# Local attention of a six-part decoder: another order of the work within each group of heads, on all four engines

## The chip, the core and the metric

One core of a Trainium2 chip runs the whole program in one launch. The metric is device time in microseconds (us), the median of the runs shown. TensorE multiplies, VectorE, ScalarE and GpSimd do the element-wise work, and SyncE only starts transfers. In the profile they are called PE (with PEld for its weight loads), DVE, ACT, POOL and SP.

## The reference, cut to what matters

Sixteen sequences of 128 tokens with 256 features pass through six layers: a recurrent mixer, grouped attention over a context, a dense and expert network, local attention (the one changed here), cross attention and a gated network. Each is added to its input after a normalisation. The local attention is:

```python
HEADS, KV_HEADS, HEAD_DIM = (16, 4, 128)
WINDOW, ROPE_THETA, EPS = (64, 10000.0, 1e-06)
q = (x @ Wq.T).reshape(B, T, H, Dh).transpose(0, 2, 1, 3)
k = (x @ Wk.T).reshape(B, T, Hkv, Dh).transpose(0, 2, 1, 3)
v = (x @ Wv.T).reshape(B, T, Hkv, Dh).transpose(0, 2, 1, 3)
q = _rms_norm(q, qn_w)
k = _rms_norm(k, kn_w)
...
q = q * cos + _rotate_half(q) * sin
k = k * cos + _rotate_half(k) * sin
q = q * Dh ** (-0.5)
scores = jnp.einsum('bhgtd,bhkd->bhgtk', qg, k)
mask = (dist >= 0) & (dist <= WINDOW)
scores = jnp.where(mask, scores, finfo.min)
att = jax.nn.softmax(scores, axis=-1)
ctx = jnp.einsum('bhgtk,bhkd->bhgtd', att, v)
out = ctx.transpose(...).reshape(B, T, H * Dh)
return out @ Wo.T
```

## The kernel before, in words

The local attention is the function `windowed`. It takes the 16 sequences t one after the other, and in each the four groups g of heads (one key head and its four query heads). Every engine runs its own program, `one(t, s, first, last)`, whose order is written out by hand. `pairs` unrolls the first two and the last two sequences and loops over the others, two per turn. The engines meet only through semaphores, and each waits in the order of its own program. I call the work of group g of one sequence "step g".

The stations of the work are these. `project` multiplies the normalised tokens by one 512-column piece of a weight matrix, in six matmuls (a high part and two low ones). A piece is called an item: v, k, or q0 to q3. Each step projects ahead, as `ahead` says: step 0 handles q2 of the same sequence, step 1 q3 and the v of the next, step 2 the k and q0 of the next, step 3 its q1. `take` (ACT) copies an item out of PSUM into `raw` and squares it into `square`. `rotate` (DVE) sums the squares into `sums` and multiplies the item by the cosine and sine tables, in one 128x512 and two 128x256 operations, into `straight` and `crossed`. `find_scale` (POOL) turns the sums into a scale by two small operations, and `join` (POOL) adds `crossed` to `straight`; for k it multiplies by the scale as well, which is why k needs its scale first. `turn_heads` (PE) transposes the four heads of an item, and `take_turned` (ACT) copies them to `q_t` or `k_t`.

`scores` (PE) adds the mask and four products of `q_t` and `k_t`. `maximum` and `shift` (DVE) give the bias, `weigh` (ACT) makes four exponentials with their sums, `invert` (DVE) takes the reciprocals, and `normalise` (POOL) multiplies the weights by them. One step later `turn_weights` (PE) transposes the weights, `take_weights` (DVE) copies them, `attend` (PE) makes the weighted sum, `take_attended` (ACT) and `split_out` (DVE) split it into `out_high` and `out_low`; yet one step later `project_out` (PE) multiplies both by a piece of the output matrix. `finish` (DVE) adds the result of a sequence to x. On DVE and PE, `normalise`, `turn_h` and `split_h` prepare the tokens of the next sequence in step 0.

The output projection of a step waits for the split of the step before:

```python
def project_out(t, g):
    pe.wait_ge(attended_taken, U * t + g + 1)
    pe.wait_ge(out_low_ready, U * t + g + 1)
```

and so does the next weighted sum, since the sum has one bank only:

```python
def attend(t, s, g):
    pe.wait_ge(turned_p_taken, U * t + g + 1)
    need(pe, attended_taken, U * t + g)
    need(pe, out_low_ready, U * t + g)
```

## Time and profile before

| what | value |
|---|---|
| median of 3 runs | 1591.7 us (1590.38 to 1596.24) |
| time of the profiled execution | 1597.39 us |
| its span | 1595.6 us |
| PE busy, of the span | 1339.1 us (84%) |
| DVE busy | 1099.5 us (69%) |
| ACT busy | 810.9 us (51%) |
| POOL busy | 629.7 us (39%) |
| mean granted clock of TensorE, of full speed | 0.929 |
| local attention, about | 751 to 1245 us from the span's start |

The busy shares are means over six layers with different limits. What the change can do must be read in the stretch of the local attention alone, in the order of time on each engine.

### The profile page before, as it was taken

How to read it: one execution, taken by the hardware profiler on the slowest of the kernel's cores; microseconds unless marked ns; L12 is line 12 of the kernel's file. 1: busy time of each engine (PE TensorE's matmuls, PEld its weight loads, DVE VectorE, ACT ScalarE, POOL GpSimd, SP SyncE). 2: the span in 40 equal slices, each digit the busy share in tenths (PEclk: the TensorE clock that was granted, in tenths of full speed). 3: DMA queues.
4: the chain of work that ended last, by engine and by line, in shares of the span. 5: the costliest groups of instructions: out<-in, count | busy, mean ns of one | idle time of the engine just before them, and what ended most of it. 6: DMA issues, size and time to landing. Idle time of an engine off the chain costs nothing. (4 is left out here: it accounts for less than half of the span.)

```text
span 1595.6 us, 26439 instructions
## 1 busy us (share of the span) xinstructions
PE 1339.1 (84%) x7985; PEld 1027.9 (64%) x8032; DVE 1099.5 (69%) x2086; ACT 810.9 (51%) x1811; POOL 629.7 (39%) x693
## 2 busy tenths in 40 slices
PE   6775278888699999984898998998998788987998
PEld 3332155555588888873677776777776465656887
DVE  5999588889456767568777777777776466653443
ACT  2222078888454343435565665665665255652332
POOL 3220466556561000006666566656665333220000
PEclk9988589999799999996999999999999799998999
DMA  9000133331000000002000000000000000000000
GB/s 367 41 0 0 40 99 87 79 79 40 1 1 1 1 0 0 1 1 96 1 1 1 0 0 0 0 0 0 0 0 1 5 3 3 2 1 1 14 13 27
DMA packets 30303, 40.24 MB, mean 25 GB/s; under 512 B 4320, under 2 KB 25824, under 8 KB 28704
## 3 DMA queue, kind: packets, MB, share of 16 engines
q1 hardware_dynamic: 30240, 39.45, 7.9%
q8 instruction: 33, 0.54, 0.1%
q14 instruction: 30, 0.25, 0.1%
HBM read 28.96 MB, written 2.10 MB: 19 GB/s over the span
## 5 line engine op out<-in xcount | busy, mean ns | idle before, releaser
L1704 ACT ACTIVATE wi_weights<-wi_psum,wi_bias,wi_scale 128x128 f32<-128x128 f32 x256 | 113.9, 454 | 113.0 <-DVE wi_bias L1814 113.0
L1479 POOL TENSOR_TENSOR wi_straight<-wi_straight,wi_crossed 128x512 f32<-128x512 f32 x80 | 110.0, 1374 | 5.8 <-DVE wi_crossed L1800 5.7
L846 DVE TENSOR_REDUCE gq_top<-gq_psum 128x4 f32<-128x512 f32 x128 | 86.8, 678 | 32.0 <-PE gq_psum L733 31.2
L1467 POOL TENSOR_TENSOR wi_scratch<-wi_sums,wi_eps 128x4 f32<-128x4 f32 x80 | 35.9, 449 | 159.7 <-DVE wi_sums L1783 158.3
L1805 DVE TENSOR_REDUCE wi_top<-wi_psum 128x4 f32<-128x512 f32 x64 | 44.0, 688 | 74.7 <-PE wi_psum L1594 74.7
L800 ACT ACTIVATE gq_weights<-gq_weights 128x512 f32<-128x512 f32 x128 | 81.1, 634 | 25.2 <-DVE gq_weights L854 23.9
L1018 POOL TENSOR_TENSOR ex_scratch<-ex_squares,ex_eps 128x4 f32<-128x4 f32 x12 | 2.4, 201 | 231.0 <-ACT ex_junk L1129 231.0
L740 PE MATMUL gq_psum<-const,gq_weights 128*128 128x128 f32 x512 | 79.3, 278 | 14.9 <-ACT gq_weights_t L806 14.9
L1215 DVE TENSOR_TENSOR ex_gated<-ex_gated,ex_psum 128x512 f32<-128x512 f32 x64 | 43.9, 687 | 65.2 <-PE ex_psum L1070 53.9
L1142 ACT ACTIVATE ex_hidden_high<-ex_gated 128x512 fp32r<-128x512 f32 x64 | 40.4, 632 | 93.8 <-DVE ex_gated L1215 93.8
L854 DVE TENSOR_TENSOR gq_weights<-gq_psum,gq_top 128x512 f32<-128x512 f32 x128 | 87.2, 681 | 0.0
L1468 POOL TENSOR_TENSOR wi_scale<-wi_scratch,minus_half 128x4 f32<-128x4 f32 x80 | 84.6, 1057 | 6.3
L806 ACT ACTIVATE gq_weights_t<-gq_psum 128x512 f32<-128x512 f32 x128 | 76.0, 594 | 12.0 <-PE gq_psum L740 11.3
L1616 PE MATMUL wi_psum<-wi_wo_high,wi_out_high 128*128 128x256 f32 x256 | 46.9, 307 | 41.7 <-DVE wi_out_low L1768 39.0
L740 PEld LDWEIGHTS gq_psum<-const,gq_weights 128*128 128x128 f32 x512 | 61.9, 142 | 29.8 <-ACT gq_weights_t L806 16.9
L1800 DVE TENSOR_TENSOR wi_crossed<-wi_raw,wi_sin_q 128x256 f32<-128x256 f32 x128 | 80.9, 671 | 0.0
L1603 PE MATMUL wi_psum<-wi_weights_t,wi_values 128*128 128x512 f32 x128 | 77.8, 694 | 0.8 <-DVE wi_weights_t L1821 0.8
L1545 PEld LDWEIGHTS wi_psum<-const,wi_straight 128*128 128x128 f32 x320 | 43.9, 155 | 49.2 <-issue 48.3
L2228 DVE TENSOR_REDUCE cr_top<-cr_psum 128x4 f32<-128x512 f32 x64 | 43.7, 682 | 45.9 <-PE cr_psum L2043 45.9
L1138 ACT ACTIVATE ex_gated<-ex_psum 128x512 f32<-128x512 f32 x64 | 38.1, 595 | 64.1 <-PE ex_psum L1070 64.0
L1594 PE MATMUL wi_psum<-wi_k_t,wi_q_t 128*128 128x128 f32 x512 | 67.5, 275 | 3.5 <-ACT wi_q_t L1695 1.4
L1489 POOL TENSOR_TENSOR wi_weights<-wi_weights,wi_inverse 128x512 f32<-128x512 f32 x64 | 66.4, 1038 | 8.9 <-remote 4.6
(339 smaller groups left out, 4086.0 us busy)
## 6 DMA issues: line engine op xcount, KB each, us to landing
gq_keys<-in_ctx_keys_dram SPq DMA_DIRECT2D x16, 512.0 KB, 3.8
gq_keys_diagonal<-gq_key_parts SPq DMA_DIRECT2D x64, 128.0 KB, 3.8
x<-in_x_dram SPq DMA_DIRECT2D x4, 512.0 KB, 9.3
gate<-in_gate_dram SPq DMA_DIRECT2D x2, 1024.0 KB, 5.5
up<-in_up_dram SPq DMA_DIRECT2D x2, 1024.0 KB, 7.5
down<-in_down_dram SPq DMA_DIRECT2D x2, 1024.0 KB, 9.3
wq<-in_wq_dram SPq DMA_DIRECT2D x1, 2048.0 KB, 19.6
wo<-in_wo_dram SPq DMA_DIRECT2D x1, 2048.0 KB, 25.5
```

Of the source, the lines that this page charges most:

```text
L740: mm = pe.transpose(ps[:, bank(unit, t, u), j * P:j * P + P], weights[:, u % RINGS, j * P:j * P + P], ident)
L800: act.activation(weights[:, u % RINGS], weights[:, u % RINGS], ACT.Exp, scale=SCALE).then_inc(weighed, 1)
L806: act.activation(weights_t[:, u % PTS], ps[:, bank(unit, t, u), :], ACT.Copy).then_inc(taken, 1)
L846: dve.tensor_reduce(top[:, u % 4, :], rows(u), AX.X, ALU.max).then_inc(topped, 1)
L854: dve.tensor_tensor(weights[:, u % RINGS].rearrange("p (j t) -> p j t", t=P), rows(u), wide(top[:, u % 4, :], [P, 4, P]), ALU.subtract).th ...
L1468: found = pool.tensor_tensor(scale[:, scale_at], scratch2[:], net.half[:, 0:4], ALU.pow)
L1479: added_up = pool.tensor_tensor(straight[:, at], straight[:, at], crossed[:, at], ALU.add)
L1489: pool.tensor_tensor(weights[:, g % 2], weights[:, g % 2], wide(inverse[:, g % 2], [P, 4, P]), ALU.mult).then_inc(normalised, 1)
L1594: mm = pe.matmul(bank[:, j * P:j * P + P], q_t[:, g % 2, j, :], k_t[:, s, g, :], start=False, stop=(j == 3), skip_group_check=True)
L1603: pe.matmul(ps[:, AV, :], values[:, s, g * DH:g * DH + DH], weights_t[:, g % 2], start=True, stop=True).then_inc(attended, 1)
L1704: act.activation(weights[:, g % 2, j, :], ps[:, SC + g % 2, j * P:j * P + P], ACT.Exp, bias=bias[:, g % 2, j:j + 1], scale=scale[:, g, j:j ...
L1800: dve.tensor_tensor(crossed[:, at, :, to], raw[:, at, :, source], over_heads(sin[:, to]), ALU.mult).then_inc(parts, 1)
```

## The change

Nothing is computed otherwise, and no instruction is added or taken away in a step; the diff moves calls within each engine's `one`, and splits two functions so that their halves can stand apart. On PE a step now begins with `scores`, then the transposes of the weights, then the projections, then the transposes of the heads, the weighted sum and the output projection. On ACT the exponentials come first, then the copies out of PSUM, and the square of a q item comes last; `take_square` is split off `take`. On DVE the maximum and the bias come first, then the copy of the transposed weights and the reciprocals, then the rotations, the split of the weighted sum, and the sum of a q item's squares last; `add_squares` is split off `rotate`. The square and its sum of a k item stay right behind its copy and its rotation. On POOL the weights' normalisation comes first, then the joins, and the scales of q items last.

```diff
--- before.py
+++ after.py
@@ -1492,14 +1492,14 @@
             def one(t, s, first, last):
                 for g in range(U):
                     items = [item for item in ahead(t, s, g, last) if item[0] != "v"]
-                    for item in items[:1]:
-                        find_scale(*item)
                     normalise(t, g)
-                    for item in items[:1]:
+                    for item in items:
+                        if item[0] == "k":
+                            find_scale(*item)
                         join(*item)
-                    for item in items[1:]:
-                        join(*item)
-                        find_scale(*item)
+                    for item in items:
+                        if item[0] == "q":
+                            find_scale(*item)
                 own.again()
 
             for name in LOW_BY_POOL[:2]:
@@ -1620,22 +1620,12 @@
 
             def one(t, s, first, last):
                 for g in range(U):
-                    items = ahead(t, s, g, last)
-                    for item in items:
-                        if item[0] != "v":
-                            project(*item)
                     scores(t, s, g)
-                    for item in items:
-                        if item[0] == "v":
-                            project(*item)
                     if g > 0 or not first:
                         pt, _, pg = earlier(t, s, g, 1, U)
                         turn_weights(pt, pg)
-                    if g > 1 or not first:
-                        pt, _, pg = earlier(t, s, g, 2, U)
-                        project_out(pt, pg)
-                    if g > 0 or not first:
-                        attend(*earlier(t, s, g, 1, U))
+                    for item in ahead(t, s, g, last):
+                        project(*item)
                     if g < 3:
                         turn_heads("q", t, g + 1)
                     elif not last:
@@ -1643,6 +1633,11 @@
                         turn_heads("q", t + 1, 0)
                     if g == 0 and not last:
                         turn_h(t + 1, 1 - s)
+                    if g > 0 or not first:
+                        attend(*earlier(t, s, g, 1, U))
+                    if g > 1 or not first:
+                        pt, _, pg = earlier(t, s, g, 2, U)
+                        project_out(pt, pg)
 
             turn_h(0, 0)
             for item in FIRST_ITEMS:
@@ -1669,11 +1664,16 @@
                 n, at = of_five(what, t, g), slot(what, g)
 
                 if what == "k":
-                    need(act, parts, 3 * (of_five("k", t - 1, 0) + 1))
+                    used = of_five("k", t - 1, 0) + 1
                 else:
-                    need(act, parts, 3 * (of_five("q", t, g - 2) + 1) if g >= 2
-                         else 3 * (of_five("q", t - 1, g + 2) + 1))
+                    used = of_five("q", t, g - 2) + 1 if g >= 2 else of_five("q", t - 1, g + 2) + 1
+                need(act, parts, 3 * used)
+                need(act, squared, used)
                 act.activation(raw[:, at].rearrange("p j d -> p (j d)"), bank, ACT.Copy).then_inc(proj_taken, 1)
+            def take_square(what, t, s, g):
+                n, at = of_five(what, t, g), slot(what, g)
                 act.wait_ge(proj_taken, of_six(what, t, g) + 1)
                 need(act, summed, n - 1)
                 act.activation(square[:, square_slot(what, t, s, g)], raw[:, at], ACT.Square).then_inc(squared, 1)
@@ -1713,12 +1713,12 @@
 
             def one(t, s, first, last):
                 for g in range(U):
-                    for item in ahead(t, s, g, last):
+                    items = ahead(t, s, g, last)
+                    weigh(t, g)
+                    for item in items:
                         take(*item)
-                    weigh(t, g)
-                    if g > 0 or not first:
-                        pt, _, pg = earlier(t, s, g, 1, U)
-                        take_attended(pt, pg)
+                        if item[0] == "k":
+                            take_square(*item)
                     if g < 3:
                         take_turned("q", t, s, g + 1)
                     elif not last:
@@ -1726,6 +1726,12 @@
                         take_turned("q", t + 1, 1 - s, 0)
                     if g == 0 and not last:
                         take_turned("h", t + 1, 1 - s)
+                    if g > 0 or not first:
+                        pt, _, pg = earlier(t, s, g, 1, U)
+                        take_attended(pt, pg)
+                    for item in items:
+                        if item[0] == "q":
+                            take_square(*item)
 
             act.wait_ge(net.in_attn1, 16 * 4)
             for name in PIECES[:2]:
@@ -1735,6 +1741,8 @@
                 take_high(name)
             for item, name in zip(FIRST_ITEMS, PIECES[6:]):
                 take(*item)
+                if item[0] != "v":
+                    take_square(*item)
                 take_high(name)
             take_turned("k", 0, 0)
             take_turned("q", 0, 0, 0)
@@ -1769,7 +1777,7 @@
                                   out_high[:, g % 2].bitcast(F32).rearrange("p j t -> p (j t)"),
                                   ALU.subtract).then_inc(out_low_ready, 1)
 
-            def rotate(what, t, s, g):
+            def add_squares(what, t, s, g):
 
                 if what == "v":
                     return
@@ -1782,6 +1790,13 @@
                     need(dve, scaled, U * t + g - 1)
                 dve.tensor_reduce(sums[:, at], square[:, square_slot(what, t, s, g)], AX.X,
                                   ALU.add).then_inc(summed, 1)
+            def rotate(what, t, s, g):
+                if what == "v":
+                    return
+                at = slot(what, g)
+                dve.wait_ge(proj_taken, of_six(what, t, g) + 1)
 
                 if what == "k":
                     need(dve, turned, number("k", t - 1) + 1)
@@ -1834,26 +1849,29 @@
 
             def one(t, s, first, last):
                 for g in range(U):
+                    items = ahead(t, s, g, last)
+                    maximum(t, g)
                     if g == 0 and not last:
                         normalise(t + 1, 1 - s)
-                    maximum(t, g)
+                    shift(t, g)
                     if g > 0 or not first:
                         pt, _, pg = earlier(t, s, g, 1, U)
                         take_weights(pt, pg)
-                    shift(t, g)
-                    items = [item for item in ahead(t, s, g, last) if item[0] != "v"]
-                    for item in items[:1]:
+                    if g == 2 and not first:
+                        finish(t - 1)
+                    invert(t, g)
+                    for item in items:
                         rotate(*item)
-                    invert(t, g)
-                    for item in items[1:]:
-                        rotate(*item)
-                    if g == 1 and not first:
-                        finish(t - 1)
+                        if item[0] == "k":
+                            add_squares(*item)
+                    if g == 0 and not last:
+                        split_h(t + 1, 1 - s)
                     if g > 0 or not first:
                         pt, _, pg = earlier(t, s, g, 1, U)
                         split_out(pt, pg)
-                    if g == 0 and not last:
-                        split_h(t + 1, 1 - s)
+                    for item in items:
+                        if item[0] == "q":
+                            add_squares(*item)
                 own.again()
 
             aggregate(dve, net, aggregated)
@@ -1885,6 +1903,7 @@
                             .broadcast_to([P, 4, P])).then_inc(tables_ready, 1)
             for item in FIRST_ITEMS:
                 rotate(*item)
+                add_squares(*item)
             for name in LOW_BY_DVE[4:]:
                 take_low(dve, name, low_dve)
             pairs(dve, one)
```

The first place is PE in step 3 of a sequence, in the unrolled sequences. In the rows, a write to `wi_psum` from `const,wi_weights` is `turn_weights`, from `const,wi_straight` `turn_heads` (x8 is k and q0 of the next sequence), from `wi_weights_t,wi_values` `attend`, from `wi_wo_...` `project_out`. Before:

```order
L1581 MATMUL wi_psum<-wi_wq_high,wi_h_high 128x512 x2
L1581 MATMUL wi_psum<-wi_wq_low,wi_h_high 128x512 x2
L1581 MATMUL wi_psum<-wi_wq_high,wi_h_low 128x512 x2
L1591 MATMUL wi_psum<-wi_mask,wi_ident 128x512
L1594 MATMUL wi_psum<-wi_k_t,wi_q_t 128x128 x4
L1559 MATMUL wi_psum<-const,wi_weights 128x128 x4
L1616 MATMUL wi_psum<-wi_wo_high,wi_out_high 128x256 x4
L1616 MATMUL wi_psum<-wi_wo_low,wi_out_high 128x256 x4
L1616 MATMUL wi_psum<-wi_wo_high,wi_out_low 128x256 x4
L1603 MATMUL wi_psum<-wi_weights_t,wi_values 128x512
L1545 MATMUL wi_psum<-const,wi_straight 128x128 x8
```

After:

```order
L1591 MATMUL wi_psum<-wi_mask,wi_ident 128x512
L1594 MATMUL wi_psum<-wi_k_t,wi_q_t 128x128 x4
L1559 MATMUL wi_psum<-const,wi_weights 128x128 x4
L1581 MATMUL wi_psum<-wi_wq_high,wi_h_high 128x512 x2
L1581 MATMUL wi_psum<-wi_wq_low,wi_h_high 128x512 x2
L1581 MATMUL wi_psum<-wi_wq_high,wi_h_low 128x512 x2
L1545 MATMUL wi_psum<-const,wi_straight 128x128 x8
L1603 MATMUL wi_psum<-wi_weights_t,wi_values 128x512
L1616 MATMUL wi_psum<-wi_wo_high,wi_out_high 128x256 x4
L1616 MATMUL wi_psum<-wi_wo_low,wi_out_high 128x256 x4
L1616 MATMUL wi_psum<-wi_wo_high,wi_out_low 128x256 x4
```

The projection of q1 has moved behind the scores, and the output projection from ahead of the weighted sum to the end of the step, behind the heads' transposes.

The second place is DVE from the rotation of k in step 2 to the first work of step 3. L1783 (L1791 after) sums squares, L1798 and L1800 (L1813, L1815) rotate, L1827 (L1842) takes the reciprocals, L1768 (L1776) splits the weighted sum, L1805 (L1820) is the maximum. Before:

```order
L1814 SCALAR_TENSOR_TENSOR wi_bias<-wi_top,wi_scale 128x4
L1783 TENSOR_REDUCE wi_sums<-wi_square 128x4
L1798 TENSOR_TENSOR wi_straight<-wi_raw,wi_cos_k 128x512
L1800 TENSOR_TENSOR wi_crossed<-wi_raw,wi_sin_k 128x4x64 x2
L1827 RECIPROCAL wi_inverse<-wi_total 128x4
L1783 TENSOR_REDUCE wi_sums<-wi_square 128x4
L1798 TENSOR_TENSOR wi_straight<-wi_raw,wi_cos_q 128x512
L1800 TENSOR_TENSOR wi_crossed<-wi_raw,wi_sin_q 128x4x64 x2
L1768 TENSOR_TENSOR wi_out_low<-wi_psum,wi_out_high 128x512
L1805 TENSOR_REDUCE wi_top<-wi_psum 128x4
```

After:

```order
L1842 RECIPROCAL wi_inverse<-wi_total 128x4
L1813 TENSOR_TENSOR wi_straight<-wi_raw,wi_cos_k 128x512
L1815 TENSOR_TENSOR wi_crossed<-wi_raw,wi_sin_k 128x4x64 x2
L1791 TENSOR_REDUCE wi_sums<-wi_square 128x4
L1813 TENSOR_TENSOR wi_straight<-wi_raw,wi_cos_q 128x512
L1815 TENSOR_TENSOR wi_crossed<-wi_raw,wi_sin_q 128x4x64 x2
L1776 TENSOR_TENSOR wi_out_low<-wi_psum,wi_out_high 128x512
L1791 TENSOR_REDUCE wi_sums<-wi_square 128x4
L1820 TENSOR_REDUCE wi_top<-wi_psum 128x4
L1829 SCALAR_TENSOR_TENSOR wi_bias<-wi_top,wi_scale 128x4
```

Before, the rotation of k stood ahead of the reciprocals; now both rotations stand behind them, and the bias of the next step follows its maximum.

The third place is POOL in steps 2 and 3. L1467 and L1468 are `find_scale`, L1489 `normalise`, L1479 and L1482 `join`. Before:

```order
L1467 TENSOR_TENSOR wi_scratch<-wi_sums,wi_eps 128x4
L1468 TENSOR_TENSOR wi_scale<-wi_scratch,minus_half 128x4
L1489 TENSOR_TENSOR wi_weights<-wi_weights,wi_inverse 128x512
L1479 TENSOR_TENSOR wi_straight<-wi_straight,wi_crossed 128x512
L1482 TENSOR_TENSOR wi_straight<-wi_straight,wi_scale 128x512
L1479 TENSOR_TENSOR wi_straight<-wi_straight,wi_crossed 128x512
L1467 TENSOR_TENSOR wi_scratch<-wi_sums,wi_eps 128x4
L1468 TENSOR_TENSOR wi_scale<-wi_scratch,minus_half 128x4
L1467 TENSOR_TENSOR wi_scratch<-wi_sums,wi_eps 128x4
L1468 TENSOR_TENSOR wi_scale<-wi_scratch,minus_half 128x4
L1489 TENSOR_TENSOR wi_weights<-wi_weights,wi_inverse 128x512
```

After:

```order
L1489 TENSOR_TENSOR wi_weights<-wi_weights,wi_inverse 128x512
L1467 TENSOR_TENSOR wi_scratch<-wi_sums,wi_eps 128x4
L1468 TENSOR_TENSOR wi_scale<-wi_scratch,minus_half 128x4
L1479 TENSOR_TENSOR wi_straight<-wi_straight,wi_crossed 128x512
L1482 TENSOR_TENSOR wi_straight<-wi_straight,wi_scale 128x512
L1479 TENSOR_TENSOR wi_straight<-wi_straight,wi_crossed 128x512
L1467 TENSOR_TENSOR wi_scratch<-wi_sums,wi_eps 128x4
L1468 TENSOR_TENSOR wi_scale<-wi_scratch,minus_half 128x4
L1489 TENSOR_TENSOR wi_weights<-wi_weights,wi_inverse 128x512
L1479 TENSOR_TENSOR wi_straight<-wi_straight,wi_crossed 128x512
L1467 TENSOR_TENSOR wi_scratch<-wi_sums,wi_eps 128x4
```

The scale of k, which stood ahead of the weights' normalisation, now stands behind it. The scale of q1 (the two rows ahead of the last L1489 before) has moved behind its join (the last row after).

## Rows read from the trace of the kernel before

**Rows 1.** Busy time by stretch: columns from:to, length, busy us by engine, granted clock, DMA.

```profile
751.00:1245.00 494.00, 438.71 (x2587) 355.97 (x2617) 356.59 (x700) 300.96 (x839) 307.01 (x317) 0.94 0.00 0
```

**Rows 2.** Waits of PE in local attention: us in total, times, longest.

```profile
PE wi_psum L1616 <- DVE wi_out_low L1768: 39.0, 15, 2.7
```

**Rows 3.** Timeline of PE: start, us, engine, line, operation xcount, idle before.

```profile
780.11 0.71 PE L1616 MATMUL wi_psum<-wi_wo_high,wi_out_high 128*128 128x256 f32 x4 [2.65 <-issue]
...
1014.86 0.72 PE L1616 MATMUL wi_psum<-wi_wo_high,wi_out_high 128*128 128x256 f32 x4
...
1017.60 0.71 PE L1581 MATMUL wi_psum<-wi_wq_high,wi_h_high 128*128 128x512 f32 x2
...
1019.08 0.39 PE L1591 MATMUL wi_psum<-wi_mask,wi_ident 128*128 128x512 bf16 x1
1019.31 1.05 PE L1594 MATMUL wi_psum<-wi_k_t,wi_q_t 128*128 128x128 f32 x8
...
1023.47 0.71 PE L1616 MATMUL wi_psum<-wi_wo_high,wi_out_high 128*128 128x256 f32 x4 [2.67 <-DVE wi_out_low L1768]
...
1028.24 0.71 PE L1581 MATMUL wi_psum<-wi_wq_high,wi_h_high 128*128 128x512 f32 x2
...
1207.46 0.71 PE L1616 MATMUL wi_psum<-wi_wo_high,wi_out_high 128*128 128x256 f32 x4 [2.70 <-DVE wi_out_low L1768]
```

**Rows 4.** Busy time and granted clock in two single microseconds, columns as in the first group.

```profile
1022.00:1023.00 1.00, 0.00 (x0) 0.00 (x0) 1.00 (x2) 0.00 (x0) 0.64 (x2) 1.00 0.00 0
1025.00:1026.00 1.00, 1.00 (x5) 0.83 (x4) 1.00 (x3) 1.00 (x7) 0.84 (x3) 0.50 0.00 0
```

**Rows 5.** Timeline of DVE, the same sequence; the last row from the last sequence.

```profile
1014.71 0.69 DVE L1805 TENSOR_REDUCE wi_top<-wi_psum 128x4 f32<-128x512 f32 x1 [2.20 <-PE wi_psum L1594]
...
1015.91 0.15 DVE L1814 SCALAR_TENSOR_TENSOR wi_bias<-wi_top,wi_scale 128x4 f32<-128x4 f32 x1
1015.98 0.68 DVE L1783 TENSOR_REDUCE wi_sums<-wi_square 128x4 f32<-128x512 f32 x1
1016.58 0.68 DVE L1798 TENSOR_TENSOR wi_straight<-wi_raw,wi_cos_k 128x512 f32<-128x512 f32 x1
1017.18 0.75 DVE L1800 TENSOR_TENSOR wi_crossed<-wi_raw,wi_sin_k 128x256 f32<-128x256 f32 x2
1018.00 0.18 DVE L1827 RECIPROCAL wi_inverse<-wi_total 128x4 f32<-128x4 f32 x1
...
1018.80 1.34 DVE L1798 TENSOR_TENSOR wi_straight<-wi_raw,wi_cos_q 128x512 f32<-128x512 f32 x1
1020.06 2.66 DVE L1800 TENSOR_TENSOR wi_crossed<-wi_raw,wi_sin_q 128x256 f32<-128x256 f32 x2
1022.65 0.68 DVE L1768 TENSOR_TENSOR wi_out_low<-wi_psum,wi_out_high 128x512 fp32r<-128x512 f32 x1
...
1229.64 0.18 DVE L1827 RECIPROCAL wi_inverse<-wi_total 128x4 f32<-128x4 f32 x1 [1.94 <-ACT wi_weights L1704]
```

**Rows 6.** Timeline of POOL, the same; last, the joins by ns minimum/median/maximum.

```profile
1016.82 0.50 POOL L1467 TENSOR_TENSOR wi_scratch<-wi_sums,wi_eps 128x4 f32<-128x4 f32 x1 [3.29 <-DVE wi_sums L1783]
...
1018.55 1.04 POOL L1489 TENSOR_TENSOR wi_weights<-wi_weights,wi_inverse 128x512 f32<-128x512 f32 x1
1019.55 1.72 POOL L1479 TENSOR_TENSOR wi_straight<-wi_straight,wi_crossed 128x512 f32<-128x512 f32 x1
1021.34 1.10 POOL L1482 TENSOR_TENSOR wi_straight<-wi_straight,wi_scale 128x512 f32<-128x512 f32 x1
...
1229.89 1.04 POOL L1489 TENSOR_TENSOR wi_weights<-wi_weights,wi_inverse 128x512 f32<-128x512 f32 x1 [3.17 <-DVE wi_inverse L1827]
...
L1479 POOL TENSOR_TENSOR wi_straight<-wi_straight,wi_crossed x80: 1263/1286/1757, 743.7 to 1225.5; 128x512 f32<-128x512 f32 x80
```

**Rows 7.** Timeline of ACT, the first exponential of a step and the copy behind four.

```profile
1016.10 0.46 ACT L1704 ACTIVATE wi_weights<-wi_psum,wi_bias,wi_scale 128x128 f32<-128x128 f32 x1 [1.17 <-DVE wi_bias L1814]
...
1017.86 0.60 ACT L1711 ACTIVATE wi_out_high<-wi_psum 128x512 fp32r<-128x512 f32 x1
```

## The prediction

> **What bounds the kernel now.** I read the stretch first: over 494 us of local attention PE is busy for 439 us, DVE 357, POOL 307, ACT 301 [rows 1]. PE is nearly the bound, and the question is where its rest goes. The waits say: 39.0 us in 15 waits of the output projection for the split of the weighted sum [rows 2], one of 2.67 us in step 3 of each sequence [rows 3]. The timelines say why. The split is queued on DVE behind two rotations (k and q0). Their multiplications have both inputs in SBUF, and so do POOL's. The 128x512 one takes 0.68 us for k but 1.34 for q0, ending 0.55 us after POOL's normalisation (18.55 + 1.04 = 19.59); the two 128x256 ones take 2.66 us instead of 0.75, beside L1479 and L1482 [rows 5, 6]. So the two engines take turns, one instruction at a time. The wait costs twice: PE stands still at full clock, then the clock falls to half [rows 4], and from 1023.47 to 1028.24 pass 4.77 us. At full clock the same work (output projection, weighted sum, eight transposes) takes 2.74 us for the piece with four transposes (1014.86 to 1017.60) plus 0.36 for four more, 3.10. Loss: 1.67 us [rows 3]. One sequence takes (1207.46 - 780.11) / 14 = 30.53 us on average [rows 3]; near 1023 about 30.6, of which 2.67 + 1.67 are the wait and the clock, and 26 to 26.3 PE's own work.
>
> **What the change does to that wait.** The output projection of a step now stands last in the next step but one and its split is a whole step older, so the 39.0 us go. If PE's own work were all, each sequence would take some 26.3 us. It isn't all, because the order on DVE and ACT becomes serial. Let M be the start of a step's maximum and W that of its first exponential.
>
> - M to W: maximum 0.69, a wait for its own result (nearest: L1479 to L1482 on POOL, 0.07; I take 0.10), bias 0.15, hand-over 0.04 (15.91 + 0.15 to 16.10): 0.98 [rows 5 to 7]. Before it was 1.39 (14.71 to 16.10), so the exponentials start 0.4 us sooner.
> - W to the copy of the projection into `raw`: 1.76; the copy 0.60, hand-over 0.04 [rows 7]. Before, this copy and the square ran ahead of the exponentials and DVE rotated meanwhile. Now the rotation begins at W + 2.40, and during the exponentials DVE has only the weights' copy (in step 2 also `finish`, which fits).
> - The reciprocals start at W + 1.90 (16.10 to 18.00), POOL's normalisation 0.25 after (1229.64 to 1229.89), at W + 2.15, until W + 3.19 [rows 5 to 7]. So it holds the turn when the rotation comes. By the 18.80 row the multiplication then ends 0.55 after it, at W + 3.74 instead of 3.08. The next starts 0.08 before an end; the pair of halves takes 0.68 to the next start: W + 4.34 [rows 5].
> - Then the split and the sum of squares, 0.60 each from start to start (15.98 to 16.58): W + 5.54. The next maximum can't start sooner.
>
> So a step of DVE takes 0.98 + 5.54 = 6.52 us; in step 0 two 128x256 operations more (`normalise`, `split_h`, bounded by half of L1800's pair, 0.35, of which the first hides half): 7.04. From M of step 0 to W of step 2: 7.04 + 6.52 + 0.98 = 14.54. PE's own share of them is less (about 26 us for four steps), so its scores come sooner: DVE and ACT bound them.
>
> In step 2 the rotation and sum of k end at W + 5.02 (4.34 + 0.68). POOL starts 0.16 later (15.98 + 0.68 to 16.82); find_scale takes 1.73 (16.82 to 18.55), the join 1.29 by its median, + 0.07, the multiplication 1.10, the join of q0 1.29 [rows 5, 6]. That is W + 10.65, with a hand-over of 0.05. Here is the new stall: PE is in step 3 after q1's projection at about W + 7.2 (ACT copies `q_t` until W + 4.2, then scores, weights' transposes, projection: 3.0) and waits to W + 9.35 for k and to W + 10.65 for q0: 2.8 us without work, four transposes between. Behind them stand the weighted sum and the output projection, then the scores on which M of the next step 0 depends: 2.74 and 1.32 (1019.08 to 1020.36, + 0.04) [rows 3].
>
> **The sum.** One sequence at full clock: 14.54 + 10.65 + 4.06 = 29.25 us, against 30.53. The moves themselves add no instruction; what they cost is that DVE now idles under the exponentials. The clock must be added. Before, 2.67 us of standing still cost 0 to 1.67 us (the wait at 780.11 was followed by full speed, 1023.47 by 1.67). The new wait is as long, and all that follows it is on the path that sets the next M. Over the stretch the clock was granted at 0.94 [rows 1], so 0.12 of 494 us ran at half, 59 us, in which 30 us were lost: 2.0 per sequence with start and end, so most waits paid in full. I take 1.2, nearer the upper bound: 30.45. Over 14 sequences -1.1 us. The first sequence gains about 1 us (scores no longer behind a projection). In the last, steps 0 and 1 take 6.5 instead of 5.7 each, and the last two gain 0.8 each, as the copy to `q_t` no longer waits for that of the weighted sum: 0. Sum -2, to which I add 2 for the hand-overs of a queue that is now serial (four per sequence, 0.03 to 0.05 each, estimated from the 0.04 above). Forecast: no change. The profiled execution, 1597.4 with its span of 1595.6, stays; the median of the runs shown is 5.7 below, and there I forecast **1592 us**.
>
> By the page "TensorE: Matmul & The Clock Gate", Part 4, transposes don't count as busy time for the clock. Then the four k transposes don't break the standing still, and the clock falls every time: 29.25 + 1.67 = 30.92 per sequence, +5 us. That is the Trainium skill; no row here tests it alone, and it moves my choice of 1.2 by nothing. The page "SBUF — State Buffer", SBUF: two separate sides, says in the Trainium skill that the shared port pair is a lock for a whole instruction, taken by whoever starts first. The trace agrees (1.34 against 0.68), and the rule speaks against this change, which puts every rotation 0.25 us behind a normalisation; were the port shared by rate, the multiplication would end after twice its 0.68, at W + 3.76, and the sum would be the same.
>
> **Rivals.**
> - The clock stays high, as the transposes of k break the wait: 29.25, so 14 x -1.28 = -18 us, 1574. For it: the wait at 780.11 cost nothing. Against: the mean of 0.94 says that most waits did cost. Chance 0.22.
> - The turn falls to DVE: if `raw` is ready before the reciprocals are through, the rotation goes first, three times 0.66 us less in 29.25, 27.3 and the wait of PE with it: 14 x -3.3, 1546. Against: 2.40 against 2.15, of which the 0.60 copy is fixed. It decides at 0.25 us. Chance 0.06.
> - Slower: L1467 of k's scale, which starts together with q0's rotation, waits for all three of its multiplications instead of one. It would then end at W + 6.3 instead of 5.7, and if a join behind it loses a turn to DVE as at 19.55 (1.72 for 1.29, 0.43) that is 1.0 us per sequence: 30.25 at full clock, 31.45 to 31.92 with the lower one, 14 x 0.92 to 1.39, or +13 to +19 us, 1605 to 1611. It decides from 0.7 us on, where the sequence reaches 31.1 us. Against: the L1467 at 16.82 took 0.50 us, beside a multiplication of DVE too, and none of DVE's is due while the joins of k run. Chance 0.18.
> - The change doesn't do what it says: the projection waits on as before. The order rules it out; 0.
>
> The forecast case (the lower clock costs 0.6 to 1.67) has 0.54; its own range is -10 to +6, 1582 to 1598.
>
> **The numbers.** 0.5% of 1592 is 8 us, about what this measurement can tell from no change. Faster by more: 0.22 + 0.06 and 0.04 of the forecast case, 0.32. Slower by more: 0.18 and 0.04 of it for mis-sized hand-overs, 0.22. Within: 0.46. The range runs from the full-clock case, 1574, to the lower end of the slow one, 1605.
>
> **What would show it.** Right: PE's wait for L1768 is gone (0 of 15), and PE waits some 2 us per sequence for POOL's L1482 and 0.6 more for L1479 before the eight transposes of step 3. DVE's 128x512 rotation takes 1.34 us in steps 0, 1 and 2 (k), 0.68 for q0 and q1. From maximum to maximum pass 7.0 us in step 0, 6.5 in step 1, 8.4 in step 2 (0.98 + 4.34 + 0.60 + 1.28 + 1.20) and the rest in step 3. DVE no longer waits 2.2 us for scores [rows 5]; ACT waits for the bias. Wrong: 128x512 rotations of 0.68 throughout, or PE's wait on another tile; or a split that now waits for ACT's copy longer than 0.3 us in every step, which would make ACT's new order the bound.

## The result and the profile after

The changed kernel took 1602.55 us (median of 17 runs, 1597.35 to 1603.35), the kernel before 1596.24 in the same comparison (17 runs, 1590.38 to 1598.15): ratio 1.0036, 95% interval 1.0025 to 1.0047. That is slower by a third of a per cent, inside the 0.5% taken as no change. The profiled execution has a span of 1600.3 us. Of the experiments below only e5 had a run in the slow state (2624.16 us), and its numbers leave that run out.

Waits in and around local attention (740 to 1260 us) of the changed kernel: us in total, times, longest.

```profile
ACT wi_weights L1704 <- DVE wi_bias L1829: 182.3, 64, 5.4
POOL wi_weights L1489 <- DVE wi_inverse L1842: 98.9, 48, 3.7
DVE wi_inverse L1842 <- ACT wi_weights L1704: 72.7, 64, 1.9
...
PE wi_psum L1545 <- POOL wi_straight L1482: 31.0, 15, 2.1
...
DVE wi_top L1820 <- PE wi_psum L1594: 25.5, 17, 5.4
...
PE wi_psum L1545 <- POOL wi_straight L1479: 10.6, 17, 1.1
```

The 39.0 us for the split [rows 2] are gone (1.5 us in one wait remain). In their place PE waits 31.0 + 10.6 us for POOL's rotated heads, and ACT, DVE and POOL wait for each other in a circle. The stretch from 751 to 1245, to be read beside [rows 1]: the clock is 0.93 for 0.94.

```profile
751.00:1245.00 494.00, 446.68 (x2606) 366.23 (x2605) 341.69 (x687) 284.29 (x839) 292.22 (x316) 0.93 0.00 0
```

DVE, timeline of steps 2 and 3 of one sequence (beside [rows 5]).

```profile
1018.16 0.68 DVE L1820 TENSOR_REDUCE wi_top<-wi_psum 128x4 f32<-128x512 f32 x1
...
1020.97 0.18 DVE L1842 RECIPROCAL wi_inverse<-wi_total 128x4 f32<-128x4 f32 x1 [0.44 <-ACT wi_weights L1704]
1021.54 1.27 DVE L1813 TENSOR_TENSOR wi_straight<-wi_raw,wi_cos_k 128x512 f32<-128x512 f32 x1 [0.40 <-ACT wi_raw L1672]
1022.73 0.75 DVE L1815 TENSOR_TENSOR wi_crossed<-wi_raw,wi_sin_k 128x256 f32<-128x256 f32 x2
1023.40 0.68 DVE L1791 TENSOR_REDUCE wi_sums<-wi_square 128x4 f32<-128x512 f32 x1
1024.00 0.68 DVE L1813 TENSOR_TENSOR wi_straight<-wi_raw,wi_cos_q 128x512 f32<-128x512 f32 x1
...
1026.46 0.68 DVE L1820 TENSOR_REDUCE wi_top<-wi_psum 128x4 f32<-128x512 f32 x1
```

POOL, the same time (beside [rows 6]).

```profile
1021.22 1.04 POOL L1489 TENSOR_TENSOR wi_weights<-wi_weights,wi_inverse 128x512 f32<-128x512 f32 x1 [1.54 <-DVE wi_inverse L1842]
1024.24 0.50 POOL L1467 TENSOR_TENSOR wi_scratch<-wi_sums,wi_eps 128x4 f32<-128x4 f32 x1 [1.98 <-DVE wi_sums L1791]
1024.82 1.06 POOL L1468 TENSOR_TENSOR wi_scale<-wi_scratch,minus_half 128x4 f32<-128x4 f32 x1
1026.04 1.27 POOL L1479 TENSOR_TENSOR wi_straight<-wi_straight,wi_crossed 128x512 f32<-128x512 f32 x1 [0.16 <-POOL wi_scale L1468]
1027.38 1.04 POOL L1482 TENSOR_TENSOR wi_straight<-wi_straight,wi_scale 128x512 f32<-128x512 f32 x1
1028.38 1.27 POOL L1479 TENSOR_TENSOR wi_straight<-wi_straight,wi_crossed 128x512 f32<-128x512 f32 x1
```

PE, behind q1's projection in step 3 (beside [rows 3]), with the weighted sum of step 2, 10 us earlier, in front for comparison.

```profile
1020.86 1.02 PE L1603 MATMUL wi_psum<-wi_weights_t,wi_values 128*128 128x512 f32 x2
...
1028.47 0.65 PE L1545 MATMUL wi_psum<-const,wi_straight 128*128 128x128 f32 x4 [2.09 <-POOL wi_straight L1482]
1029.70 1.05 PE L1545 MATMUL wi_psum<-const,wi_straight 128*128 128x128 f32 x4 [0.57 <-POOL wi_straight L1479]
1030.55 1.91 PE L1603 MATMUL wi_psum<-wi_weights_t,wi_values 128*128 128x512 f32 x2
1031.47 1.84 PE L1616 MATMUL wi_psum<-wi_wo_high,wi_out_high 128*128 128x256 f32 x4
```

The granted clock over two single microseconds, in the wait and behind it (beside [rows 4]): 2.4 GHz, then 1.2.

```profile
1027.00:1028.00 1.00, 0.00 (x0) 0.00 (x0) 0.91 (x3) 0.63 (x3) 0.92 (x2) 1.00 0.00 0
1031.00:1032.00 1.00, 1.00 (x3) 0.33 (x1) 0.21 (x1) 0.47 (x1) 1.00 (x2) 0.50 0.00 0
```

What to see: the chain of step 2 is as forecast. The normalisation holds the turn at 1021.22, so k's rotation takes 1.27 us; its sum ends at 1024.08, the scale and two operations of POOL follow, and PE gets k at 1028.47, 2.09 us after it had nothing left. The same weighted sum takes 1.91 us behind the wait, 1.02 before it.

Where the time is. I cut both profiled spans at the first L1755/L1763 (`h_tok`) of local attention, at the maximum of step 0 in sequences 1 and 15, and at the last `finish`. Readings, before and after: first `h_tok` 729.36, 728.15; maximum of sequence 1 786.07, 789.02; of sequence 15 1215.07, 1219.87; `finish` 1242.76, 1249.92. So the prologue and first sequence cost +4.2 us, fourteen sequences +1.8 (429.00 to 430.85), the last one +2.4. Ahead of attention the changed kernel was 1.2 shorter, and behind it 2.5 (352.84 to 350.38). Sum +4.7, as the spans say. Local attention by itself grew by 8.4 us. This cut is useful for the experiments, since the part ahead of attention ended between 723.97 and 730.61 in all fourteen profiles with no edit there. In the table **attention** is first `h_tok` to last `finish`, **sequence** the mean from one `h_tok` to the next over thirteen sequences, and the clock that of 780 to 1200 us.

| kernel | ratio to before (95%) | attention | sequence | clock |
|---|---|---|---|---|
| before | 1 | 513.4 | 30.58 | 0.95 |
| changed | 1.0036 (1.0025, 1.0047) | 521.8 | 30.79 | 0.94 |
| e1_no_norm | 0.9785 (0.9757, 0.9812) | 477.2 | 27.99 | 1.00 |
| e2_after_fill | 0.9907 (0.9880, 0.9935) | 497.2 | 29.27 | 1.00 |
| e3_pe_only | 1.0221 (1.0196, 1.0246) | 549.2 | 32.82 | 1.00 |
| e4_rest_only | 0.9956 (0.9940, 0.9972) | 504.8 | 29.60 | 1.00 |
| e5_before_split | 0.9892 (0.9859, 0.9925) | 498.7 | 29.57 | 0.96 |
| e6_both_rot | 0.9827 (0.9796, 0.9857) | 486.1 | 28.71 | 1.00 |
| e7_invert_late | 1.0033 (1.0018, 1.0048) | 518.2 | 30.72 | 0.94 |
| e8_before_fill | 0.9862 (0.9832, 0.9893) | 491.1 | 29.15 | 1.00 |
| e9_rot_shift | 0.9835 (0.9815, 0.9856) | 487.4 | 28.88 | 1.00 |
| e10_first_old | 1.0005 (0.9992, 1.0017) | 517.1 | 30.60 | 0.95 |
| e11_norm_first | 0.9750 (0.9730, 0.9770) | 476.4 | 27.98 | 1.00 |
| e12_norm_shift | 0.9734 (0.9715, 0.9752) | 470.0 | 27.84 | 1.00 |

### The profile page after: what moved, and what is told of

Its sections match the earlier page's. It is cut to its first block and busy times, and to the rows that moved or that the text cites. A ratio compares the mean times of both kernels' runs of the same rounds, so it can differ in the third digit from the quotient of the medians.

```text
span 1600.3 us, 26563 instructions
## 1 busy us (share of the span) xinstructions
PE 1346.1 (84%) x8032; PEld 1035.0 (65%) x8032; DVE 1086.2 (68%) x2086; ACT 793.9 (50%) x1811; POOL 615.7 (38%) x693
## 5 line engine op out<-in xcount | busy, mean ns | idle before, releaser
L1479 POOL TENSOR_TENSOR wi_straight<-wi_straight,wi_crossed 128x512 f32<-128x512 f32 x80 | 103.5, 1294 | 43.7 <-DVE wi_crossed L1815 41.5
L1489 POOL TENSOR_TENSOR wi_weights<-wi_weights,wi_inverse 128x512 f32<-128x512 f32 x64 | 66.5, 1039 | 104.7 <-DVE wi_inverse L1842 98.9
L1545 PE MATMUL wi_psum<-const,wi_straight 128*128 128x128 f32 x320 | 54.2, 296 | 51.1 <-POOL wi_straight L1482 31.0
L1468 POOL TENSOR_TENSOR wi_scale<-wi_scratch,minus_half 128x4 f32<-128x4 f32 x80 | 89.4, 1118 | 6.3
L1545 PEld LDWEIGHTS wi_psum<-const,wi_straight 128*128 128x128 f32 x320 | 39.9, 149 | 68.4 <-POOL wi_straight L1482 37.5
L1616 PE MATMUL wi_psum<-wi_wo_high,wi_out_high 128*128 128x256 f32 x256 | 77.9, 433 | 1.5 <-DVE wi_out_low L1776 1.5
L1813 DVE TENSOR_TENSOR wi_straight<-wi_raw,wi_cos_q 128x512 f32<-128x512 f32 x64 | 63.7, 995 | 17.3 <-ACT wi_raw L1672 17.3
L2247 DVE TENSOR_REDUCE cr_top<-cr_psum 128x4 f32<-128x512 f32 x64 | 43.7, 682 | 44.5 <-PE cr_psum L2062 44.5
L1616 PEld LDWEIGHTS wi_psum<-wi_wo_high,wi_out_high 128*128 128x128 f32 x256 | 46.7, 224 | 40.3 <-issue 38.0
L1594 PEld LDWEIGHTS wi_psum<-wi_k_t,wi_q_t 128*128 128x128 f32 x512 | 69.6, 197 | 1.8
```

Source lines behind the costliest of these rows:

```text
L1468: found = pool.tensor_tensor(scale[:, scale_at], scratch2[:], net.half[:, 0:4], ALU.pow)
L1479: added_up = pool.tensor_tensor(straight[:, at], straight[:, at], crossed[:, at], ALU.add)
L1545: mm = pe.transpose(ps[:, bank_of(what, g), j * P:j * P + P], straight[:, slot(what, g), j, :], ident)
L1616: mm = pe.matmul(ps[:, OUT, 0:D], out[:, g % 2, j, :], w[:, j, :], start=(g == 0 and n == 0 and j == 0), stop=(g == 3 and n == 2 and j == ...
```

## Experiments on the two halves and on the clock

**e1: the normalisation made tiny.** It normalises 4 columns of the weights only, so the rest of the weights go into the sum undivided.

```diff
-pool.tensor_tensor(weights[:, g % 2], weights[:, g % 2], wide(inverse[:, g % 2], [P, 4, P]),
+pool.tensor_tensor(weights[:, g % 2, 0, 0:4], weights[:, g % 2, 0, 0:4], inverse[:, g % 2],
```

> The changed kernel, with GpSimd's normalisation of the weights cut from 128x512 to 128x4 elements (the softmax weights stay undivided, the rest is computed as before). Theory (turns at the port): the first 128x512 rotation of steps 0, 1 and 2 no longer waits 0.6 us for its turn and takes 0.68 us; all three lie on the path, so a sequence takes 30.77 - 1.75 = 29.0 us and the kernel 26 us less than the changed one, about 1576. Rival (TensorE and its clock set the period, the turns are hidden in slack): rotations shorter, time within 4 us of the changed kernel.

Measured 1560.79 us, sequence 27.99. The q rotations' 128x512 multiplications, and PE's two waits in one sequence:

```profile
L1813 DVE TENSOR_TENSOR wi_straight<-wi_raw,wi_cos_q 128x512 f32<-128x512 f32 x59 | 40.7, 690 | 16.1 <-ACT wi_raw L1672 16.1
```

```profile
1005.44 0.66 PE L1545 MATMUL wi_psum<-const,wi_straight 128*128 128x128 f32 x4 [0.97 <-POOL wi_straight L1482]
...
1006.66 0.66 PE L1545 MATMUL wi_psum<-const,wi_straight 128*128 128x128 f32 x4 [0.56 <-POOL wi_straight L1479]
```

The long rotations are gone (0.69 us each), so it is the normalisation beside them that makes them long. A sequence gains 2.8 us, 1.0 more than I expected: the wait for k is 1.1 us shorter, and the clock, which I had left out, stays at 2.4 GHz over it. Next to the changed kernel at full clock (29.27 in e2, below) the edit itself is worth 1.3 us, where I had expected 1.75.

**e2: the changed kernel with fill.** Dummy multiplications occupy PE where it waits for k and q0. They write half a bank whose other half holds the output's sum, and disturb it.

```diff
+    fill(15)
     turn_heads("k", t + 1, 0)
+    fill(4)
     turn_heads("q", t + 1, 0)
```

> The changed kernel, with 15 unused 128x256 matmuls ahead of k's transposes in step 3 and 4 ahead of q0's, into half a PSUM bank that nothing reads: 1.8 and 0.5 us of work inside a wait of 2.1 and 0.6. Theory (the low clock behind the wait lies on the path): the granted clock stays at 1.0, a sequence takes 29.3 instead of 30.77, the kernel 20 to 22 us less, about 1581. Rival (VectorE bounds the steps whatever the clock): within 5 us of the changed kernel. If the fill itself delays the transposes, a sequence grows by up to 0.3 us.

Measured 1578.32 us, a sequence of 29.27, clock 1.00. PE does more work and the kernel is 1.3% faster than the changed one. The fill doesn't hold up the heads (PE still waits 0.34 us for k behind it, and q0's transposes start 1.24 us behind k's, 1.23 without fill), so what changed is the clock, and it costs the changed kernel 30.79 - 29.27 = 1.52 us a sequence.

**e8: the kernel before with fill**, ahead of step 3's output projection. It writes the bank of the projections once ACT has copied q0 out of it, so nothing reads it.

```diff
+                        if g == 3 and not last:
+                            fill(t, s, 19)
                         project_out(pt, pg)
```

> The kernel before, with 19 added multiplications of 128x256 on TensorE ahead of the output projection of step 3, where it waited 2.7 us for the split; they write a bank that nothing reads, and compute nothing that is kept. Theory (prediction, clock: behind this wait the granted clock is 1.2 GHz for a while, and this costs the kernel before about as much as its wait in step 3 costs the changed one): the clock is 2.4 GHz in the whole loop, a sequence goes from 30.6 to 29.0 us, the kernel to 1568 to 1573 us. Rival: in the kernel before VectorE's queue hides the low clock: within 5 us of before.

Measured 1571.24 us, a sequence of 29.15, clock 1.00. PE still waits 0.42 us for the split behind the fill. The kernel before lost 30.58 - 29.15 = 1.43 us a sequence to the clock. Side by side at full clock: 29.15 before, 29.27 after; on top of it 1.43 and 1.52.

**e3 and e4: each half of the change alone.** e3 is the kernel before with PE's new order only; e4 the changed kernel with PE's old order, so only DVE's, ACT's and POOL's are new.

The edit is the diff's hunks in PE's `one`, in e3 applied alone, in e4 taken back alone. Its core, as in e3:

```diff
-                    for item in items:
-                        if item[0] != "v":
-                            project(*item)
                     scores(t, s, g)
...
-                        project_out(pt, pg)
-                    if g > 0 or not first:
-                        attend(*earlier(t, s, g, 1, U))
+                    for item in ahead(t, s, g, last):
+                        project(*item)
```

> The kernel before, with only TensorE's order changed (scores first, projections behind them, output projection last). Theory (the four orders belong together): ScalarE still copies and squares the projection ahead of the exponentials and now waits for it, so W moves from about scores + 1.4 to + 3.2 and more (two items in step 2); steps of 7.4, 8.1, 8.8 and 7.4 us, 31.7 per sequence, 16 us slower than before, about 1612. Rival (the wait for the split is all, and TensorE's new order removes it): 39 us of waits and the low clock go, 30 to 60 us faster than before.

> The changed kernel, with only TensorE's order of before (projection, scores, output projection, weighted sum, heads' transposes last). Theory (VectorE's serial order bounds steps 0 to 2, and behind q0's join stand on TensorE only what follows the transposes): 14.5 + 10.65 us as before, then transposes 0.36, the next projection 1.48 and the scores 1.32 instead of 4.06: 28.3 at full clock, 29 to 29.9 with part of the loss, 13 to 25 us faster than the changed kernel, 1578 to 1590. Rival (it is TensorE's new order that holds the time down): slower than the changed kernel by more than 8 us.

Measured 1629.19 and 1584.92 us. The waits that grew, from 780 to 1200 us, of e3 and then of e4:

```profile
ACT wi_raw L1671 <- PE wi_psum L1581: 167.2, 51, 3.4
...
PE wi_psum L1591 <- ACT wi_q_t L1690: 34.9, 25, 1.5
```

```profile
PE wi_psum L1616 <- DVE x L1851: 22.0, 14, 1.6
```

By itself PE's new order is the harmful half. ACT still takes the projection ahead of the exponentials and now waits for it behind the scores; 2.2 us a sequence are lost although no clock is (1.00), more than the 1.1 that I expected. The other half alone is a gain of 0.4%. At full clock the picture is another one: 29.15 us a sequence before, 29.60 with the other half alone, 29.27 with both. So the other half gains by the clock only, and on top of it PE's new order saves 0.33 us and loses 1.52 to the clock. My sum for e4 was wrong all the same: I expected 28.3 us and a loss by the clock; the trace has 29.60 and none, because PE's waits there are 1.6 us (for `finish`, which now stands in step 2) and the clock stays at 2.4 GHz behind them.

## Experiments on whose turn it is

**e7: the rotation ahead of the reciprocals**, in the changed kernel.

```diff
-                    invert(t, g)
-                    for item in items:
+                    for item in items[:1]:
                         rotate(*item)
+                    invert(t, g)
```

> The changed kernel, with one edit of VectorE's program: the reciprocals stand behind the first rotation of the step instead of ahead of it, so that the rotation comes ahead of POOL's normalisation. Theory: the first rotations of steps 0, 1 and 2 take 0.68 instead of 1.27 us, a sequence goes from 30.8 to 28.0 us where the clock stays at 2.4 GHz and to 29.5 where it still falls in step 3: 1560 to 1583 us. Rival: TensorE waits for the later weights by as much as VectorE gains: within 5 us of the changed kernel, 1593 to 1603.

Measured 1599.2 us (10 runs), ratio 1.0033: no gain over the changed kernel. DVE's row shows that the edit did what it should (the rotation takes 0.69 us), POOL's and PE's what became of it:

```profile
1012.98 0.69 DVE L1820 TENSOR_REDUCE wi_top<-wi_psum 128x4 f32<-128x512 f32 x1 [0.63 <-PE wi_psum L1594]
...
1016.39 0.69 DVE L1813 TENSOR_TENSOR wi_straight<-wi_raw,wi_cos_k 128x512 f32<-128x512 f32 x1 [1.02 <-ACT wi_raw L1672]
```

```profile
1017.92 1.04 POOL L1489 TENSOR_TENSOR wi_weights<-wi_weights,wi_inverse 128x512 f32<-128x512 f32 x1 [3.44 <-DVE wi_inverse L1842]
1018.92 0.65 POOL L1467 TENSOR_TENSOR wi_scratch<-wi_sums,wi_eps 128x4 f32<-128x4 f32 x1
```

```profile
1005.71 0.66 PE L1559 MATMUL wi_psum<-const,wi_weights 128*128 128x128 f32 x4 [0.51 <-POOL wi_weights L1489]
...
1023.33 0.66 PE L1545 MATMUL wi_psum<-const,wi_straight 128*128 128x128 f32 x4 [1.51 <-POOL wi_straight L1482]
```

k's sum is ready earlier, but POOL now does the normalisation when it comes, and starts k's scale 5.94 us after the maximum (1012.98 to 1018.92) instead of 6.08 (1018.16 to 1024.24). From maximum to k's transposes pass 10.35 us, in the changed kernel 10.31. k's rotation and the normalisation (1.04 us) both stand ahead of k's scale, in either order, so this edit moves the delay and doesn't remove it; in step 1 the later normalisation makes PE wait 0.51 us. The edit does more than swap the turn: the reciprocals stand behind all three operations of the rotation, so the normalisation starts 4.94 us after the maximum instead of 3.06. The rival of the prediction (turn falls to DVE, the normalisation later by one multiplication only) is therefore not tested by e7.

**e5: the split ahead of the second rotation**, in the kernel before.

```diff
-                    for item in items[1:]:
-                        rotate(*item)
                     if g == 1 and not first:
                         finish(t - 1)
...
                         split_out(pt, pg)
+                    for item in items[1:]:
+                        rotate(*item)
```

> The kernel before, with one edit of VectorE's program: the second rotation of a step moves from ahead of finish and the split of the sums to behind them. Theory (step (a) of the prediction: TensorE's wait of 39.0 us for the split, 2.7 us in 15 sequences, is on the path, but what VectorE has behind it, its own queue, is what bounds the sequence next): the wait goes, and about half of it comes back as VectorE work behind, so a sequence goes from 30.6 to about 29.2 us, and the kernel to 1570 to 1580 us. Rival: TensorE alone bounds it, and the whole wait with the low clock behind it goes: 26.3 us for a sequence, about 1530 us. Second rival: the wait only changes its name (the next heads or the next projection wait by as much), within 5 us of before.

Measured 1578.65 us, a sequence of 29.57: 1.0 us gained, 0.4 less than I expected. The wait for the split is gone, but a shorter one stands in its place, and the clock falls behind it too (PE's row, then one microsecond with columns as in [rows 1]):

```profile
1016.81 1.70 PE L1603 MATMUL wi_psum<-wi_weights_t,wi_values 128*128 128x512 f32 x2 [1.91 <-DVE wi_weights_t L1821]
...
1018.00:1019.00 1.00, 1.00 (x5) 0.70 (x4) 0.93 (x4) 1.00 (x5) 0.84 (x3) 0.50 0.00 0
```

The rotation that was ahead of the split is now ahead of the next copy of the weights. So 1.0 us is what this exchange is worth, and not what the wait of 2.67 us with its clock costs.

**e6: both rotations ahead of the reciprocals**, in the kernel before, so that the normalisation doesn't meet q0's rotation.

```diff
-                    for item in items[:1]:
+                    for item in items:
                         rotate(*item)
                     invert(t, g)
-                    for item in items[1:]:
-                        rotate(*item)
```

> The kernel before, with one edit of VectorE's program: both rotations of a step stand ahead of the four reciprocals, so that POOL's normalisation, which they release, no longer runs beside a rotation. Theory (the long rotations, 1.3 us in place of 0.68, come from POOL's operation taking the turn on the port that it shares with VectorE; who is let go first decides): every first rotation takes about 0.68 us and a sequence loses 3 us, 30.6 to about 27.6, in all about 45 us: 1545 to 1555 us. Rival: the reciprocals come 1.4 to 2 us later, and TensorE's transposes of the weights, which wait for the normalisation, give all of it back: within 5 us of before or slower.

Measured 1566.71 us, a sequence of 28.71 at a clock of 1.00. The direction is right, the size (27.6) isn't: next to 29.15 for the kernel before at full clock only 0.44 us come from the order itself; the other 1.43 are the clock, since no wait of PE in a sequence of the loop is longer than 0.8 us.

**e9: the bias ahead of the weights' copy as well.** This moves `shift` ahead of `take_weights` in e6.

> The kernel before with two edits of VectorE's program: both rotations of a step ahead of the reciprocals (the kernel that ran at 0.9827 of before), and the bias (shift) ahead of the copy of the transposed weights. Theory: in that kernel TensorE's idle time in a sequence of 28.7 us is 0.77, 0.19, 0.52 and 0.50 us, of which the 0.52 (for ScalarE's q_t, queued behind the exponentials) goes when the exponentials start about 1 us earlier, and part of the others: 28.0 to 28.4 us a sequence, the kernel at 1552 to 1562 us. Rival: the exponentials are not on the chain, VectorE's and TensorE's queues are, so nothing moves: within 3 us of that kernel, 1564 to 1570. Rival on the other side: the copy of the weights, 0.1 us later in the queue behind the bias, and the bias beside POOL's operations (1.0 us where they meet) make it later: above 1570.

Measured 1569.44 us, a sequence of 28.88: nothing gained. The earlier bias meets POOL's join behind the normalisation (L1479, 1008.31 to 1009.59) and ends with it:

```profile
1008.38 1.23 DVE L1814 SCALAR_TENSOR_TENSOR wi_bias<-wi_top,wi_scale 128x4 f32<-128x4 f32 x1
...
1010.72 1.76 DVE L1798 TENSOR_TENSOR wi_straight<-wi_raw,wi_cos_q 128x512 f32<-128x512 f32 x1
```

**e11 and e12: POOL's scale of a q behind the normalisation**, in e6 and in e9.

```diff
-                    for item in items[:1]:
-                        find_scale(*item)
+                    for item in items[:1]:
+                        if item[0] == "k":
+                            find_scale(*item)
                     normalise(t, g)
...
+                    for item in items:
+                        join(*item)
+                        if item[0] == "q":
+                            find_scale(*item)
```

> The kernel before with two edits: both rotations of a step ahead of the reciprocals (that kernel ran at 0.9827 of before, 28.7 us a sequence), and on POOL the scale of a q, 1.3 to 1.7 us of small operations, behind the normalisation and the join instead of ahead of them (that of k stays ahead). Theory: of TensorE's four short waits in a sequence two are for POOL's normalisation (0.77 and 0.50 us at the transposes of the weights), and it stood behind such a scale, at 1007.94 to 1009.20 after reciprocals that ended at 1007.42; so the 0.50 goes and perhaps the 0.77: 27.9 to 28.3 us a sequence, 1550 to 1560 us for the kernel. Rival: an earlier normalisation meets VectorE's next 128x512 operations and lengthens them, and the later scale holds the next bias: no gain, 1564 to 1572, or slower.

> The same, and the bias ahead of the copy of the transposed weights on VectorE, which with POOL's old order gave nothing (0.9835 beside 0.9827), because the earlier bias met POOL's normalisation and took 1.2 to 1.3 us in place of 0.16. Theory: with the normalisation earlier the two no longer meet, and the earlier exponentials count: 27.4 to 28.1 us a sequence, 1545 to 1558. Rival: the scale of q, now last on POOL, is what the bias waits for, and the order of the two on VectorE makes no difference: within 3 us of the kernel above.

Measured 1554.02 and 1552.0 us, sequences of 27.98 and 27.84: 2.5% and 2.7% faster than before, the best of all; the intervals of the two overlap. All waits of PE in one sequence of e11:

```profile
1000.56 0.65 PE L1559 MATMUL wi_psum<-const,wi_weights 128*128 128x128 f32 x4 [0.76 <-POOL wi_weights L1489]
...
1004.14 0.66 PE L1545 MATMUL wi_psum<-const,wi_straight 128*128 128x128 f32 x4 [0.19 <-POOL wi_straight L1479]
...
1006.49 0.39 PE L1591 MATMUL wi_psum<-wi_mask,wi_ident 128*128 128x512 bf16 x1 [0.32 <-ACT wi_q_t L1695]
```

The order of a q on POOL is also in the change; there PE waits for k, whose scale stands behind the normalisation, and no run shows what q's place is worth.

**e10: what runs once, in its old order.** The changed kernel, with PE's old order in the first sequence and, in the prologue, this:

```diff
             for item in FIRST_ITEMS:
-                rotate(*item)
                 add_squares(*item)
+                rotate(*item)
```

> The changed kernel with two edits that touch only what runs once: TensorE's order in the first sequence is that of before, and in the prologue the sums of squares stand ahead of their rotations again. From the first token-normalised heads to the first maximum of sequence 1 the traces show 56.7 us before and 60.9 after. Theory: the 4.2 us are made of these two (first heads 2.7 us later behind k's sums and beside POOL's and VectorE's halves of the weights; TensorE's 4.05 us wait for q_t in the second step), so the stretch comes to 56.5 to 58.5 us and the kernel gains 2 to 4 us on the changed one: ratio to before 1.0010 to 1.0025. Rival: the loss comes from ScalarE's and POOL's new order (exponentials ahead of the next heads), which stay: above 60 us, ratio 1.0036 as the changed kernel.

Measured 1594.28 us (12 runs), ratio 1.0005: as before within the interval. PE and DVE of the changed kernel at the start of attention show the two places:

```profile
748.25 1.09 PE L1545 MATMUL wi_psum<-const,wi_straight 128*128 128x128 f32 x4 [9.46 <-issue]
...
761.73 0.61 PE L1591 MATMUL wi_psum<-wi_mask,wi_ident 128*128 128x512 bf16 x1 [4.05 <-ACT wi_q_t L1695]
```

```profile
756.49 2.31 DVE L1829 SCALAR_TENSOR_TENSOR wi_bias<-wi_top,wi_scale 128x4 f32<-128x4 f32 x1
```

From the first `h_tok` to the first transposes of heads pass 20.10 us in the changed kernel (728.15 to 748.25), 17.36 before, and 17.38 in e10 (723.97 to 741.35): the sums behind the rotations cost 2.7 us there. To the maximum of sequence 1 pass 56.7 before, 60.9 after, 58.6 in e10, so 2.3 of the 4.2 us are gone; the sequence behind it gained another 1.5 (29.07 us in place of 30.55). The gain is a little more than I expected.

The run has both edits, but e4 helps to tell them apart: it has PE's old order with the changed prologue. From the first `h_tok` to the maxima of the first sequence, and to that of sequence 1:

| kernel | step 0 | step 1 | step 2 | step 3 | sequence 1 |
|---|---|---|---|---|---|
| before | 23.7 | 30.7 | 42.0 | 50.6 | 56.7 |
| changed | 26.5 | 36.0 | 43.7 | 52.0 | 60.9 |
| e4 | 28.1 | 36.1 | 44.1 | 52.4 | 58.8 |
| e10 | 24.5 | 34.6 | 44.1 | 52.4 | 58.6 |

And the eight transposes at the end of the first sequence, in e10 and then in e4, 54.93 and 54.87 us after the first `h_tok`:

```profile
778.90 1.34 PE L1545 MATMUL wi_psum<-const,wi_straight 128*128 128x128 f32 x8
...
779.41 1.34 PE L1545 MATMUL wi_psum<-const,wi_straight 128*128 128x128 f32 x8
```

So the 2.7 us of the prologue are there at the first transposes and absorbed by step 2, at least where PE has its old order; no run has the old prologue under PE's new one in the changed kernel. By step 3 some 1.5 to 1.9 us are lost in each kernel with the new order of DVE, ACT and POOL. The rest comes in the passage from step 3 to sequence 1: 8.85 us in the changed kernel, 6.1 before, 6.4 in e4 and 6.2 in e10. That is PE's new order, which has the weighted sum and the output projection ahead of the next scores.

## Why the prediction was right, and where it was off

The outcome (no change within 0.5%) and the range (1574 to 1605) held; the forecast of 1592 was 10.5 us below the median, and the median lies outside the range of the forecast case (1582 to 1598). 4.5 of the 10.5 are the reference: I set the forecast 5.7 us under the profiled execution because the median of three runs was 1591.7, and seventeen gave 1596.24. The other 6 are what the change cost beyond my sum. There is luck in the outcome: in the profiles attention grew by 8.4 us, 0.53% of the kernel, and the parts without an edit were 3.7 us shorter.

- **The split's wait goes, POOL's join takes its place.** Right: 39.0 us became 1.5, and PE waits 2.09 + 0.57 us per sequence for L1482 and L1479, where about 2 and 0.6 were forecast.
- **DVE and ACT become serial.** Right: from maximum to maximum the changed kernel takes 7.12, 6.54 and 8.30 us; forecast 7.04, 6.52, 8.4. Rotations of 1.26 to 1.36 us in steps 0 to 2 (forecast 1.34) and 0.68 for q0 and q1. The split waits for ACT's copy in step 3 only (1.92 us), so the sign that ACT's new order is the bound did not come.
- **A sequence at full clock, 29.25.** Right: 29.27 in e2. (Added up again with the hand-over that it names, the branch of k and q0 comes to W + 10.71 and not 10.65.)
- **The clock, 1.2 us taken between 0 and 1.67.** Mis-sized: 1.52 in the changed kernel, so 0.32 x 14 = 4.5 us too little. With it the first rival (the clock stays high) is out. The transposes of k did not break the wait here: 2.09 us idle, four of them, 0.57 idle, and the clock is down during the second four (1.05 us for 0.65). By the Trainium skill, "TensorE: Matmul & The Clock Gate", Part 4, transposes don't count as busy time, which gave 30.92 a sequence; measured were 30.8. The trace agrees with that outcome, though no run here tests transposes alone.
- **+2 us for serial hand-overs.** Wrong: at full clock there is nothing left for them (29.27 against 29.25 without). These 2 us made up for part of what the other terms lacked.
- **First sequence -1 us.** Wrong, the failed step: +4.2 with the prologue. I counted the projection that no longer stands ahead of the scores, and left out two things. The first sequence ends with the same step 3 as the others (8.85 us to the next maximum instead of 6.1), and steps 0 to 2 don't pay it back there. And what runs once moves too: in the prologue k's sums wait for the rotation, and the bias of step 0 takes 2.31 us beside POOL's 128x1024 operations on the weights, with the next heads queued behind its exponentials. By step 3 the changed kernel is 1.5 us behind the one before, and e10, with the old prologue, 1.9.
- **Last sequence 0.** Off: +2.4. Steps 0 and 1 were right (6.46 and 6.43 for 5.66 and 5.61), but step 2 took 6.83 for 5.61 instead of gaining 0.8, and step 3 gained 0.5.
- **The slower rival.** Its cost did not come: L1467 of k's scale took 0.50 us in a sequence of the loop, and no join there more than 1.30.
- **The turn on the port.** The mechanism is right: e1 brings every rotation to 0.69 us, and in e7 the rotation that comes first takes 0.69. The Trainium skill, "SBUF — State Buffer", SBUF: two separate sides, calls the shared port pair a lock for a whole instruction; the trace agrees here too, down to a bias of four columns that takes 1.23 us instead of 0.16. The price of a turn won, 27.3 us a sequence, is open. The nearest run is e1, which has no normalisation at all and reaches 27.99; e7 gives nothing, but holds back the normalisation for longer.

Where the gain went: at full clock the order of before needs 29.15 us and the new one 29.27, each with one wait of 2.1 to 2.7 us in step 3 that brings the clock down for another 1.4 to 1.5. One wait was exchanged for another of about the same size and the same second price. The 2.5 us by which the part behind attention was shorter (350.4 us in the changed kernel and in e10, 352.2 to 354.2 in the other twelve) stay open.
